# Windowed attention on one Trainium2 core: queries and keys produced column-wise and placed by DMA instead of transposed on TensorE

## The reference

```
x = x + attn0(layernorm(x))     # linear attention, one head of 64
x = x + moe0(layernorm(x))      # 8 experts, 2 per token, and a shared one
x = x + attn1(layernorm(x))     # 16 heads of 16, window +-128
x = x + moe1(layernorm(x))      # 8 experts, 1 per token, hidden 1024
```

```
q, k, v = (layernorm(x) @ W.T + b) as [batch, 16 heads, 512, 16]
energy  = q @ k.T ; energy = -max where |i - j| > 128
att     = softmax(energy / 16)
out     = (att @ v) @ Wp.T + bp
```

## Time and profile before

| | us |
|---|---|
| median of 3 runs (lowest, highest) | 1742.17 (1740.83, 1747.94) |
| the profiled execution, its own time | 1745.72 |
| span of its trace | 1744.0 |
| TensorE busy, in records | 1580.1 |
| VectorE busy | 794.9 |
| ScalarE busy | 511.1 |
| GpSimd busy | 423.2 |

### The profile page before, as it was taken

How to read it: one execution, slowest core, us unless ns; L and a number is a source line. 1 busy time by engine, 2 the same in 40 slices (tenths; PEclk the granted TensorE clock), 3 DMA queues, 4 the chain that set the end, 5 groups by cost and what they waited for, 6 DMA issues and landing times.

```text
span 1744.0 us, 23797 instructions
## 1 busy us (share of the span) xinstructions
PE 1580.1 (91%) x7755; PEld 1023.6 (59%) x7755; DVE 794.9 (46%) x2490; ACT 511.1 (29%) x891; POOL 423.2 (24%) x505
## 2 busy tenths in 40 slices
PE   5999999999999998488989798989899759999998
PEld 3666655557777776255555455645455426767676
DVE  4545333633333333567666766666666242121212
ACT  1111111111211111146555555545456201111111
POOL 1000000012222221424242423232323113333332
PEclk8999999999999999668879997979899669999999
DMA  9100010002212221100010000101022721111111
GB/s 343 44 25 24 13 36 0 1 15 61 61 61 61 63 64 48 37 13 25 13 37 28 22 31 19 34 17 37 13 73 71 252 87 49 49 46 50 44 52 22
DMA packets 60276, 89.19 MB, mean 51 GB/s; under 512 B 7389, under 2 KB 49375, under 8 KB 60160
## 3 DMA queue, kind: packets, MB, share of 16 engines
q1 hardware_dynamic: 46464, 54.73, 9.4%
q0 software_dynamic: 12096, 32.13, 6.6%
q10 hardware_dynamic: 1600, 0.81, 0.2%
HBM read 61.56 MB, written 27.00 MB: 51 GB/s over the span
## 4 chain that ended last, share of the span: by engine, by line
PE 79%; DVE 8%; issue 4%; ACT 3%; DMA 3%; POOL 2%; DVEq 0%; POOLq 0%; ACTq 0%
PE psum L602 10%; PE psum L484 10%; PE psum L787 8%; PE psum L763 8%; PE psum L581 5%; PE psum L657 5%; PE psum L495 5%; PE psum L619 4%; PE psum L644 4%; PE psum L679 4%; PE psum L633 2%; PE psum L411 2%; DMA c_got<-results,slot_of 2%; PE psum L774 2%; PE psum L421 2%
## 5 line engine op out<-in xcount | busy, mean ns | idle before, releaser
L1407 DVE CUSTOM_DVE_ANT_0 work<-psum,mask 128x384 bf16<-128x384 f32 (+1 forms) x512 | 227.5, 486 | 71.1 <-PE psum L619 69.5
L929 ACT ACTIVATE arena<-psum 128x512 f32<-128x512 f32 (+1 forms) x256 | 180.3, 706 | 221.8 <-PE psum L633 221.3
L1496 POOL DMA_INDIRECT work<-normed,token_of x110 | 104.2, 948 | 440.7 <-PE psum L563 241.9
L602 PE MATMUL psum<-arena,work 128*128 x568 | 187.4, 473 | 2.8 <-ACT work L866 2.4
L484 PE MATMUL psum<-arena 128*128 128x512 f32 (+1 forms) x384 | 174.7, 597 | 0.0
L619 PE MATMUL psum<-kT,qT 48*128 48x384 f32 (+1 forms) x512 | 127.1, 452 | 19.6 <-DVE small L1407 17.9
L787 PE MATMUL psum<-arena,work 128*128 x312 | 142.8, 601 | 1.2 <-ACT work L866 1.2
L763 PE MATMUL psum<-arena,work 128*128 x624 | 141.2, 379 | 1.9 <-DVE work L1455 1.9
L602 PEld LDWEIGHTS psum<-arena,work 128*128 128x128 f32 x568 | 103.1, 191 | 54.4 <-issue 6.1
L619 PEld LDWEIGHTS psum<-kT,qT 48*128 48x128 f32 x512 | 62.4, 208 | 112.5 <-issue 53.1
L1448 DVE TENSOR_TENSOR work<-psum,work 128x256 f32<-128x256 f32 x39 | 16.6, 425 | 243.5 <-PE psum L763 243.5
(11 more groups left out here) (172 smaller groups left out, 2322.0 us busy)
## 6 DMA issues: line engine op xcount, KB each, us to landing
arena<-in_w SPq DMA_DIRECT2D x16, 1024.0 KB, 8.5
results<-work SPq DMA_DIRECT2D x71, 128.0 KB, 1.7
normed<-work SPq DMA_DIRECT2D x16, 512.0 KB, 3.5
X<-in_x SPq DMA_DIRECT2D x8, 512.0 KB, 10.0
resid<-X SPq DMA_DIRECT2D x8, 512.0 KB, 2.9
arena<-in_wg SPq DMA_DIRECT2D x2, 1408.0 KB, 13.3
arena<-in_wu SPq DMA_DIRECT2D x2, 1408.0 KB, 14.2
arena<-in_wd SPq DMA_DIRECT2D x2, 1024.0 KB, 13.5
```

The lines of the kernel that those rows point to most:

```text
L602: m = e.matmul(psum[:, pair[u], 0:INTER], xsT0[:, b % 2, c * P:(c + 1) * P], wu0[:, bass.ds(x, 1), c, u * INTER:(u + 1) * INTER], start=(c ...
L929: e.activation(pT[:, j, 2 * half:2 * half + 2, 0:w], psum[:, bk:bk + 2, 0:w], ACT.Exp, scale=1.0 / E ** 0.5).then_inc(p_exped, 1)
L1407: e.tensor_tensor_reduce(masked[:, n % 2, 0:w], psum[:, bank_of["scores", u, i, hd], 0:w], mask[:, P - off:P - off + w], 1.0, MASKED, ALU. ...
```

## The change

Queries and keys are made column-wise: the weights are the stationary operand and the normalised columns the moving one, so that a bank holds 128 features by 512 tokens (`pe_qk`, four banks per batch; c is the half of the features, i is 0 for k and 1 for q). `pe_v` makes the values as before. ScalarE adds the bias and writes `hi`, VectorE writes `lo`. Both tiles are single: `hi[:, i, :]` holds one half of the heads at a time. From them SP places each unit by 18 DMAs from SBUF to SBUF (`sp_place`): 12 of 16 partitions into `kz`, 6 of 32 partitions into `qT`. A slot has two heads' queries under each other (96 rows) and, for each head, keys whose other head's rows are zero, so a matmul contracts over 96 rows (100 with the maxima) instead of 48 (50). There are four slots. The zeros and ones are written once, by GpSimd, among the experts of layer 0 (`pool_key_pads`). The maxima are split in two small tiles, transposed by four TensorE instructions to 8 rows (`pe_maxima`), copied (`act_maxima`) and placed by two DMAs of 4 partitions (`sp_place_maxima`).

The banks are divided: 0 to 2 for scores, 3 and 4 for `pe_again`, 5 for values, 6 and 7 for all else. Where the window is 256 wide, two heads share a bank. `pe_again` comes one step later (7), the values in pairs of tiles (steps 10 and 12). The experts' weights wait until the last `pe_again` (expert 0) and the last values (1 to 6), and are issued ahead of the last stores of X and of the normalised rows; expert 7 comes last.

```diff
-SLOT = 64
-ROWS_S, ROWS_T = 3 * DH, 3 * DH + 2
+PAIR = 2 * DH
+ROWS_S, ROWS_T = 3 * PAIR, 3 * PAIR + 4
+SLOTS = 4
 EPS = 1e-5
...
+def qk_due(step):
+    return spread(step, (-7, -5, 1, 3))
+def v_due(step):
+    return spread(step, (-6, -2, 2, 6))
...
+def values_due(step):
+    return [(u, 0) for u, _ in unit(step, 10, 1)] + [(u, 1) for u, _ in unit(step, 12, 1)]
...
+        kz = over("kz", 17408, [P, SLOTS, G, N], F32R)
+        qT = over("qT", 25600, [P, SLOTS, G // 2, N], F32R)
+        hi = over("hi", 0, [P, 2, N], F32R)
+        lo = over("lo", 1024, [P, 2, N], F32R)
+        max_T = over("max_T", 2048, [P, N], F32R)
+        max_parts = over("max_parts", 2560, [P, TPB, G, 2], F32R)
...
+        PLACED = 3 * (G + G // 2)
         A_RING, H_RING = (6, 7), ((2, 3), (4, 5))
-        S_RING, O_BANK = (0, 1, 2, 3, 4, 5, 6), 7
+        S_RING, AGAIN, O_BANK, M_RING = (0, 1, 2), (3, 4), 5, (6, 7)
...
-        def pe_scores(e, u, i, hd):
-            b, g = divmod(u, NG)
-            lo, hi = window(i)
-            p, r = 2 * g + hd // 2, SLOT * (hd % 2)
-            bk = next_of(S_RING)
-            fill(e, ("scores", u, i, hd), bk)
-            if i == 0 and hd == 0:
-                e.wait_ge(kT_made, 2 * (u + 1))
-                e.wait_ge(qT_made, 2 * (u + 1))
-            e.matmul(psum[:, bk, 0:hi - lo], qT[r:r + ROWS_S, p, i * P:(i + 1) * P], kT[r:r + ROWS_S, p, lo:hi],
...
+        def pe_scores(e, u, i, half):
+            slot = u % SLOTS
+            lo_key, hi_key = window(i)
+            w = hi_key - lo_key
+            if i == 0 and half == 0:
+                e.wait_ge(qk_placed[slot], 16 * PLACED * (u // SLOTS + 1))
...
+                m = e.matmul(psum[:, bk, at:at + w], qT[0:ROWS_S, slot, half, i * P:(i + 1) * P],
+                             kz[0:ROWS_S, slot, hd, lo_key:hi_key], start=True, stop=True)
...
+                e.wait_ge(max_placed, 16 * 2 * (u + 1))
+            for k in range(2):
+                hd = 2 * half + k
+                if w > 2 * P:
+                    bk, at = AGAIN[k], 0
+                else:
...
+                m = e.matmul(psum[:, bk, at:at + w], kz[0:ROWS_T, slot, hd, j * P:(j + 1) * P],
+                             qT[0:ROWS_T, slot, half, lo_q:hi_q], start=True, stop=True)
...
+        def pe_maxima(e, u):
+            bk = next_of(M_RING)
+            fill(e, ("maxima", u), bk)
+            e.wait_ge(maxima_made, 2 * (u + 1))
+            for t in range(TPB):
+                m = e.transpose(psum[0:2 * G, bk, t * P:(t + 1) * P],
+                                max_parts[:, t, :, :].rearrange("p h s -> p (h s)").bitcast(F32), ident[:, :])
+            m.then_inc(bank_full[bk], 1)
...
+        def pe_qk(e, b, c, i):
...
+            n0 = (1 - i) * E + c * P
+            for k in range(EC):
+                m = e.matmul(psum[:, bk, :], w_qkv[:, k, n0:n0 + P], xnT[:, xs, k, :], start=(k == 0), stop=(k == EC - 1))
+            m.then_inc(bank_full[bk], 1)
...
-                for u, j in unit(s, 6, 4):
+                for u, j in unit(s, 7, 4):
                     pe_again(e, u, j, 0)
...
-                for u, _ in unit(s, 4, 1):
-                    e.wait_ge(maxima_made, 2 * (u + 1))
-                    pe_columns(e, "q2", q_rows[:, u // NG % 2], u, 0)
-                    pe_columns(e, "q2", q_rows[:, u // NG % 2], u, 1)
...
-                for u, _ in unit(s, -2, 1):
-                    b, g = divmod(u, NG)
-                    e.wait_ge(hi_made, TPB * (b + 1))
-                    e.wait_ge(lo_made, TPB * (b + 1))
-                    pe_columns(e, "k", k_rows, u, 0)
-                    pe_columns(e, "k", k_rows, u, 1)
-                for u, _ in unit(s, -1, 1):
-                    pe_columns(e, "q", q_rows[:, u // NG % 2], u, 0)
-                    pe_columns(e, "q", q_rows[:, u // NG % 2], u, 1)
-                for b, _ in batch(s, 25):
+                for b, t in qk_due(s):
+                    pe_qk(e, b, *divmod(t, 2))
+                for b, t in v_due(s):
+                    pe_v(e, b, t)
...
+                for u, _ in unit(s, 4, 1):
+                    pe_maxima(e, u)
+                for u, i in values_due(s):
+                    pe_values(e, u, 2 * i)
+                    pe_values(e, u, 2 * i + 1)
...
+        def act_maxima(e, u):
+            if u > 0:
+                e.wait_ge(max_placed, 16 * 2 * u)
+            e.wait_ge(*done["maxima", u])
+            e.activation(max_T[0:2 * G, :], psum[0:2 * G, bank_of["maxima", u], :], ACT.Copy).then_inc(max_T_made, 1)
...
-        def act_high(e, b, t):
-            q_in, k_in, qv, kv = row_parts(b, t)
-            twice = lambda v: v.rearrange("p h (o d) -> p h o d", o=1).broadcast_to([P, H, 2, DH])
-            if t == 0:
-                rows_free(e, b)
-                e.wait_ge(pads_made, 1)
-            e.wait_ge(qk_made, TPB * b + t + 1)
-            e.activation(qv[:, :, 0:3:2, :], twice(q_in), ACT.Copy)
-            e.activation(kv[:, :, 0:2, :], twice(k_in), ACT.Copy).then_inc(hi_made, 1)
+        def act_high(e, b, c, i):
+            for u in (NG * b + 2 * c - 2, NG * b + 2 * c - 1):
+                if u >= 0:
+                    e.wait_ge(qk_placed[u % SLOTS], 16 * PLACED * (u // SLOTS + 1))
+            if qk_number(b, c, i) == 0:
+                e.wait_ge(bias_loaded, 16 * 4)
+            e.wait_ge(*done["qk", b, c, i])
+            e.activation(hi[:, i, :], psum[:, bank_of["qk", b, c, i], :], ACT.Identity,
+                         bias=b_qk[:, i, c:c + 1]).then_inc(hi_made, 1)
...
-            e.tensor_tensor(qk[:, t % 2, :], psum[:, bank_of["qk", b, t], :], b_qkv[:, 0:2 * E],
-                            ALU.add).then_inc(qk_made, 1)
...
-            e.tensor_tensor(qv[:, :, 1, :], q_in, qv[:, :, 0, :].bitcast(F32), ALU.subtract)
-            e.tensor_tensor(kv[:, :, 2, :], k_in, kv[:, :, 0, :].bitcast(F32), ALU.subtract).then_inc(lo_made, 1)
...
+        def dve_low(e, b, c, i):
+            e.wait_ge(hi_made, qk_number(b, c, i) + 1)
+            e.scalar_tensor_tensor(lo[:, i, :], psum[:, bank_of["qk", b, c, i], :], b_qk[:, i, c:c + 1],
+                                   hi[:, i, :].bitcast(F32), ALU.add, ALU.subtract).then_inc(lo_made, 1)
...
-            e.tensor_scalar(rows_of[:, :, :, ROWS_S], m_in, -1.0, None, ALU.mult).then_inc(maxima_made, 1)
+            e.tensor_scalar(max_parts[:, :, :, 0], m_in, -1.0, None, ALU.mult).then_inc(maxima_made, 1)
...
+        def sp_place(e, u):
+            b, g = divmod(u, NG)
+            slot, row = u % SLOTS, G * DH * (g % 2)
+            if u == 0:
+                e.wait_ge(key_pads_made, SLOTS)
+            if u >= SLOTS:
+                e.wait_ge(*done["again", u - SLOTS, TPB - 1, G - 1])
+            e.wait_ge(hi_made, qk_number(b, g // 2, 1) + 1)
+            e.wait_ge(lo_made, qk_number(b, g // 2, 1) + 1)
+            for part, (k_from, q_from) in enumerate(((hi, hi), (hi, lo), (lo, hi))):
+                for hd in range(G):
+                    at, src = PAIR * part + DH * (hd % 2), row + DH * hd
+                    e.dma_start(kz[at:at + DH, slot, hd, :].bitcast(F32), k_from[src:src + DH, 0, :].bitcast(F32)).then_inc(qk_placed[slot], 16)
+                for half in range(G // 2):
+                    at, src = PAIR * part, row + PAIR * half
+                    e.dma_start(qT[at:at + PAIR, slot, half, :].bitcast(F32), q_from[src:src + PAIR, 1, :].bitcast(F32)).then_inc(qk_placed[slot], 16)
+        def sp_place_maxima(e, u):
+            e.wait_ge(max_T_made, u + 1)
+            for half in range(G // 2):
+                e.dma_start(qT[ROWS_S:ROWS_T, u % SLOTS, half, :].bitcast(F32), max_T[4 * half:4 * half + 4, :].bitcast(F32)).then_inc(max_placed, 16)
         def sp_expert(e, x):
-            if x < 2:
-                e.wait_ge(*done["q2", NG * (B - 2 + x) + NG - 1, 1])
-            if x == 2:
-                e.wait_ge(*done["k", NU - 1, 1])
...
+                for u, _ in unit(s, -4, 1):
+                    sp_place(e, u)
+                for u, _ in unit(s, 4, 1):
+                    sp_place_maxima(e, u)
...
-                for step, xs in ((-12, (0,)), (-2, (2,)), (2, (1,)), (6, (3, 4)), (11, (5, 6, 7))):
+                for step, xs in ((7, (0,)), (9, tuple(range(1, NX - 1))), (20, (NX - 1,))):```

TensorE, in the middle of the phase where one batch is being made and another finished. Names: `q_rows`, `k_rows` before the transposes, `qT`, `kT` behind them; the last numbers are output partitions by columns. Before:

```order
L619 MATMUL psum<-kT_52,qT_51 128x384 x2
L633 MATMUL psum<-qT_51,kT_52 128x256 x2
L657 MATMUL psum<-ident,k_rows_50 128x128 x8
L619 MATMUL psum<-kT_52,qT_51 128x384 x2
L633 MATMUL psum<-qT_51,kT_52 128x256 x2
L644 MATMUL psum<-arena 32x384 x4
L619 MATMUL psum<-kT_52,qT_51 128x256 x2
L633 MATMUL psum<-qT_51,kT_52 128x384 x2
L657 MATMUL psum<-ident,q_rows_49 128x128 x8
L619 MATMUL psum<-kT_52,qT_51 128x256 x2
L633 MATMUL psum<-qT_51,kT_52 128x384 x2
```

334 lines of the change are left out of this document (157 added, 177 removed).

## The result

The changed kernel takes 1794.69 us (median of 4 runs, 1791.85 to 1798.29) where the kernel before takes 1741.5: a ratio of 1.0305, 95% interval 1.0263 to 1.0348. It is slower by 3%. The forecast was 1662 us, faster, and the time lies above the range too. The profiled execution spans 1796.6 us, 52.6 more than the 1744.0 of before.

A forecast was written before the change was run, and what follows sets the result against it. TensorE was taken to bound the kernel, at clock 0.895. Per batch 82.6 - 16.6 - 4.0 + 4 + 2 + 2 = 70.0 us; 1745.7 - 88 + 8 = 1665.7, median 3.5 lower: 1662 us, range 1600 to 1735.

The forecast's parts named there:

- SP's queue, +2 (bounds 0 and 5): New wait for DMA placements of queries and keys, issues at 0.41 us: +2 us a batch, one placement 1.7 us late.
- The rival's inequality, 6 steps >= 38d + 3.7: Limit on step time if SP bounds, d being the issue price: 3.2 us a step at d = 0.41.
- SP becomes the bound, 0.08: Rival: DMA issues at 0.8 us make SP's queue set the step at 5.7 us; 1817 us, chance 0.08.
- The maxima, counted on TensorE alone: Maxima's 16 small transposes at 0.136 us each: +2.2 us a batch on TensorE.
- TensorE's terms: Transposes, maxima, values and score bursts on TensorE: 14.9 us a batch saved at full clock, 16.6 at 0.895.
- A burst of two and two: Two 384-wide and two 256-wide score matmuls, one after the other, hold the array 0.59 us instead of 0.70.
- The borders' idle time: Idle time around paired score matmuls goes; bursts gain 0.11 us at 20 places, -2.2 us a batch.
- `pe_again` waits: With two banks, `pe_again` waits for the last pair's exponential: +4 us a batch, bounds 0 and 8.
- The wait for L1418, -4.0: TensorE's wait for VectorE's L1418, writing maxima into slots 64 apart, goes: -4.0 us a batch.
- The fetch, +2: VectorE's wait for fetched rows (c_got) grows as steps shorten: +2 us a batch, at most +5.5.
- The clock rises, 0.17: Rival: without column transposes TensorE's granted clock goes from 0.895 to 1.0; 1619 us, chance 0.17.
- Seven batches and +8 at the ends: The batch gain counts seven times, -88 us; pipeline fill, later `pe_again` and normalised rows behind expert weights add 8 us.

The follow-up runs named there:

- experiment 1: Changed kernel with two tiles each of hi and lo, one for each half of the heads; 1714.41 us, ratio 0.9822.
- ninth experiment: Kernel before the change plus seven groups of six test DMAs on SP; an issue costs 0.62 to 0.63 us SBUF to SBUF; one run, 1774.37 us.
- third experiment: Changed kernel with two tiles each of hi and lo and the store of X two steps later; 1707.94 us, ratio 0.9771.
- fifth experiment: The third experiment's kernel with the two DMAs of the maxima issued by ScalarE instead of SP; 1658.96 us, ratio 0.9544.
- sixth: The third experiment's kernel with weight rows permuted, 9 larger DMAs a unit instead of 18, a batch's four products close together; 1687.64 us, ratio 0.97.
- seventh experiment: The sixth's kernel with the maxima's DMAs issued by ScalarE; 1705.0 us, ratio 0.9798.
- eighth experiment: Kernel before the change, each score matmul over all 128 rows of a pair of heads instead of its own 48 or 50; 1718.12 us, ratio 0.9879.

## Why the prediction was wrong

- **SP's queue, +2 (bounds 0 and 5): the step that failed.** The issue was priced at 0.41 us, after two DMAs of which each has one end in DRAM, and 0.41 was taken over to a kind of which the trace had none. It is 0.62. The prediction had said what that means: from 0.60 it eats into the forecast. But that is the smaller part. The rival's inequality, 6 steps >= 38d + 3.7, gives 4.5 us a step with 0.62, 73 us a batch, 3 more than the forecast's 70; measured are 84.2. The batch from 1063.69 to 1146.68, 83.0 us, adds up like this. Its 76 issues take 49.2 us, where the inequality has 47.1. Twice, the way leads from the last issue of a half to `hi` (2.8 together) and from there over two steps to the next placement (12.29, 1076.45 to 1088.74, and 11.43); these take 26.6, where it has 25.6. The store of X takes 7.2, most of it waiting in the queue with SP otherwise ready, where it has nothing. The store's wait was seen, but costed as 1.7 us of lateness of one placement, not as time of a queue that had become the bound. The experiments agree: with the store two steps later the kernel is 45 us faster, and with two tiles, so that the engines no longer wait for this queue, about 80.
- **SP becomes the bound, 0.08: the case that came true,** by its own mark (a placement's issues over 0.6 us, ScalarE's waits for DMAs over 5 us a batch: 50.9 in 400 us, some 11 a batch) and with its mechanism; its price of 0.8 us an issue was too high and its time, 1817, too. By its inequality alone the kernel would be slower than before only from 0.72; it was slower at 0.62, since the store's wait was not in it. The sentence from the Trainium skill beside it (DMA: Bandwidth & Descriptors, Bandwidth: transfers under 64 KB are descriptor-dominated) pointed at the right term for a reason that does not hold for issuing: in the ninth experiment 1 KB and 256 KB cost the same.
- **The maxima, counted on TensorE alone.** That their DMAs stand in SP's queue behind a placement was shown in the order of the instructions, and no term priced it. It cost 22.0 us of waits of TensorE's loads in 289 us of the third experiment, and the fifth gained 40 to 49 us by taking it away.
- **TensorE's terms: right in their sum.** The fifth experiment has them all, without SP's chain, and a batch takes 64.6 us. The forecast's 70.0 at a clock of 0.895 are 66.0 at the 0.965 that it was granted (its 55.7 us of work become 51.7). The parts fit less well: TensorE's records are busy for 58.0 us, 6 more than that, and it is idle for 6.6, where 14.3 were counted. As records overlap, no run tells which of the two is off. A burst of two and two takes 0.56 us, by the estimate above, where 0.59 was forecast and 0.70 measured before. The borders' idle time without releaser in front of the scores fell from 26.5 us to 19.3 in four batches, 1.8 a batch where 2.2 were forecast (for the whole burst). `pe_again` waits 3.2 us a batch by its matmuls and 5.0 by its loads, forecast 4.
- **The wait for L1418, -4.0: right.** Its successor L1432 writes into a compact tile in 0.215 us on average, and TensorE waits 0.4 us in four batches for it in the fifth experiment (in the sixth and seventh it is back, 11.8 and 10.3 us in 300).
- **The fetch, +2: wrong sign.** The waits for c_got fell from 4.4 to 0.7 us a batch in the fifth experiment.
- **The clock rises, 0.17: half true.** In the changed kernel it is 0.86, with TensorE busy 77% of a batch; where SP doesn't hold it, 0.965. But the rule cited for it was not needed. The Trainium skill (TensorE: Matmul & The Clock Gate, PE-mode transpose) says of a transpose that "it doesn't count as PE-busy the same way", and the eighth experiment keeps all of them and is granted 0.97. Giving up the pairs in half the array was enough. The Trainium skill's advice to put small contractions in separate row groups (TensorE: Matmul & The Clock Gate, Why this matters for your kernels) does not pay in this kernel. Giving it up would cost 8.5 us a batch by the prediction's estimate; the unpaired scores gain 4.7, about half of it, by an estimate, with the clock.
- **Seven batches and +8 at the ends: mis-sized, and opposite in sign.** In the fifth experiment the six middle batches gain 104.8 us (490.5 to 385.7) and the first and last together nothing (63.4 and 56.7 to 59.2 and 60.4): before, those two did not hang on TensorE in the same way. The normalised rows behind the weights cost 11.8 us, not 3: with some MB of weights on their way each further weight DMA took SP up to 4.6 us to issue, so that the store was issued only at 1446.67, 36 us after the last `pe_again`, and then landed late.

That the fifth experiment lands at 1659 beside a forecast of 1662 is partly luck: a clock and a fetch better than assumed pay for the first batch and the tail.

## What to carry to other kernels

Before work is moved from a compute engine to many small DMAs, count the issues: the queue's time per unit (here 18 x 0.63 = 11.3 us) against the unit's own time. Add every wait that stands in that queue, since it counts in full once the queue is the bound. An issue's price is read from a DMA with the same two ends, or is an open bound that must reach to the point where the verdict turns. A small DMA that someone waits for (the maxima, the normalised rows) belongs on another queue, or ahead of the long ones, where the trace shows that wait (the seventh experiment had none left to take away), and a tile that DMAs read needs a second buffer.
